# The second stage's weight jobs issued in the group that uses them, and another table of scores with O's second half transposed in the ninth step

## The reference

```
s = attention(xn)          # 32 heads of 16, q and k layer-normed, ALiBi slopes, causal, softmax, output projection
g = silu(ffn(xn))          # (silu(xn @ Wg) * (xn @ Wu)) @ Wd, inner size 1792
out = x + s * g            # Wg, Wu, Wd are integers 0..15: (w - zero) * scale per group of 128 rows
```

## Time and profile before

| | |
|---|---|
| three timed runs | 1124.39, 1126.78 (median), 1127.07 us |
| the profiled execution | 1119.51 us, of which the span 1117.7 us lies between its first and last instruction |
| PE, DVE, ACT, POOL busy over the span | 1039.0, 933.7, 722.6, 465.6 us |
| second stage, first to last exponentials | 193.0 to 705.3 us |
| mean granted clock of TensorE | 0.978 of 2.4 GHz |

### The profile page before, as it was taken

The page is one execution under the profiler, slowest core; times in us unless marked ns, Lnnn a source line. Parts: engine busy times, 40 slices in busy tenths (PEclk is TensorE's granted clock), DMA queues, the critical chain, the costliest instruction groups (busy, mean ns, idle before and its releaser), DMA issues. The chain is left out here.

```text
span 1117.7 us, 18980 instructions
## 1 busy us (share of the span) xinstructions
PE 1039.0 (93%) x6242; PEld 639.5 (57%) x6242; DVE 933.7 (84%) x2162; ACT 722.6 (65%) x1152; POOL 465.6 (42%) x554
## 2 busy tenths in 40 slices
PE   5999987998999999989999999899999999999995
PEld 4788764433344343433444333577778778777874
DVE  6778897887888787878889885579989998998896
ACT  3666655675767666666667668567747766774774
POOL 2566545221111111111121112039946864994686
PEclk9999999999999998999999999899999999999997
DMA  6254862543544544464454343100120011012001
GB/s 214 70 158 137 220 149 78 154 123 64 142 109 109 129 78 97 90 142 109 95 125 94 103 87 106 39 1 0 40 75 1 1 49 66 1 39 76 1 1 38
DMA packets 98584, 95.32 MB, mean 85 GB/s; under 512 B 28030, under 2 KB 80950, under 8 KB 98486
## 3 DMA queue, kind: packets, MB, share of 16 engines
q1 hardware_dynamic: 96854, 93.72, 32.7%
q10 hardware_dynamic: 1632, 0.39, 0.2%
HBM read 72.45 MB, written 21.23 MB: 84 GB/s over the span
## 5 line engine op out<-in xcount | busy, mean ns | idle before, releaser
L896 ACT ACTIVATE pr<-pair 128x1024 f32<-128x1024 f32 (+3 forms) x384 | 296.6, 813 | 168.1 <-PE pair L1017 90.7
L279 DVE CUSTOM_DVE_ANT_0 bank<-bank,sg 128x384 f32<-128x384 f32 (+3 forms) x488 | 231.4, 517 | 73.4 <-PE bank L289 72.1
L1538 PE MATMUL pair<-xc_lo,w_gu 128*128 128x512 f32 x448 | 182.6, 408 | 4.1 <-DVE xc_lo L1374 4.1
L1539 PE MATMUL pair<-xc_hi,w_gu 128*128 128x512 f32 x448 | 176.5, 394 | 0.0
L282 DVE TENSOR_REDUCE mx<-bank 128x1 f32<-128x512 f32 x240 | 150.5, 684 | 6.0 <-PE bank L289 3.7
L1386 DVE SCALAR_TENSOR_TENSOR gate<-pair,sgu,gate 128x512 f32<-128x512 f32 x168 | 124.5, 741 | 27.0 <-PE pair L1539 25.4
L1177 POOL TENSOR_TENSOR yt<-yt,tmp 128x512 f32<-128x512 f32 x96 | 124.2, 1314 | 0.0
L289 PE MATMUL bank<-ks,qs 108*128 108x512 bf16 (+3 forms) x384 | 116.2, 335 | 5.6 <-DMA ks<-in_krows 5.0
L1012 PE MATMUL pair<-s_sb,xin_c 111*128 111x512 bf16 (+3 forms) x384 | 97.8, 338 | 12.0 <-DMA s_sb<-dt 9.2
L289 PE MATMUL bank<-xin_c,s_sb 108*128 108x512 bf16 (+3 forms) x344 | 106.0, 341 | 3.1 <-DMA xin_c<-in_krows 3.0
L1012 PE MATMUL pair<-qs,ks 111*128 111x512 bf16 (+3 forms) x384 | 97.1, 337 | 12.7 <-DMA qs<-dt 11.0
(11 more groups left out here) (122 smaller groups left out, 2166.5 us busy)
## 6 DMA issues: line engine op xcount, KB each, us to landing
stk<-parts SPq DMA_DIRECT2D x16, 768.0 KB, 5.7
zst<-in_z_all SPq DMA_DIRECT2D x24, 448.0 KB, 4.0
sst<-in_w_all SPq DMA_DIRECT2D x24, 448.0 KB, 5.7
xin_c<-in_x SPq DMA_DIRECT2D x32, 256.0 KB, 3.3
s_sb<-stk SPq DMA_DIRECT2D x96, 64.0 KB
xin_c<-stk SPq DMA_DIRECT2D x96, 64.0 KB
qs<-stk SPq DMA_DIRECT2D x96, 64.0 KB
ks<-stk SPq DMA_DIRECT2D x96, 64.0 KB
```

The lines of the kernel that those rows point to most:

```text
L279: dve.tensor_tensor_reduce(out=src, in0=src, in1=tri[:, 512 - w:512], scale=1.0, scalar=-3.0e38, op0=ALU.add, op1=ALU.max, accum_out=dst). ...
L896: act.activation(pr[e % 3][:, 2 * p:2 * p + 2, 0:w], pair[p][:, :, 0:w], ACT.Exp, scale=SCALE)\
L1538: pe.matmul(GB[j % 4], w, xc_lo[:, k, :], start=True, stop=False)
L1539: pe.matmul(GB[j % 4], w, xc_hi[:, k, :], start=False, stop=True).then_inc(gu_done, 1)
```

## The change

Three things change, all in the second stage. The table `PLAN` is another one: the group's own pieces come first, D1 moves from the first place of the eleventh step to the last of the tenth, O0 from the fourth step to the last place of the ninth, O1 from the tenth step to the twelfth, and five small pieces stand in the group's very last place. The weight jobs move: each group `i > 0` issues the pair of job `3 ip + s` at its start on SP, and an odd group after it that of job `3 ip + 2`, in front of its loads; the conversions stand in front of the fourth step's exponentials, and in odd groups also in front of the ninth's; POOL's jobs follow. And since `ot` is now still waiting for its transposes when the upper half's output is finished, `copy_o` of the upper half waits for O0.

```diff
         PLAN = (
-            "4u 5u 3", "4u", "6u",
...
+            "2 2", "2", "4u",
...
+            "", "O1", "0 0 1 1 0",
...
-        JOB_AT, JOB1_AT = 6, 2
+        JOB_AT, JOB2_AT = 3, 8
...
                 def body(i, s, ip, last):
-                    if s == 1:
-                        half_job(ip, 2)
-                    if not last:
-                        half_job(*((ip, 1), (ip + 1, 0))[s])
-                    else:
+                    if i > 0:
+                        half_job(ip, s)
+                    if last:
...
+                    if s == 1:
+                        half_job(ip, 2)
                     if last is None:
...
                 def body(i, s, ip, last):
-                    if s == 1:
-                        job(ip, 1)
-
                     pool.wait_ge(m_free, number(i, of_kind["own"][-1]) + 1)
...
-                    job(ip, (0, 2)[s])
+                    job(ip, s)
...
+                    if s == 1:
+                        job(ip, 2)
...
                 def copy_o(i, k):
-
+                    if k == 0 and i > 0:
+
+                        act.wait_ge(m_full, number(i, "O0") + 1)
...
-                        if e == JOB1_AT and s == 1:
-                            convert(ip, 1)
                         if e == JOB_AT:
-                            convert(ip, (0, 2)[s])
+                            convert(ip, s)
+                        if e == JOB2_AT and s == 1:
+                            convert(ip, 2)
```

More of the change, by code:

```diff
@@ L217, in build @@
         PLAN = (
-            "4u 5u 3", "4u", "6u",
[L219 to L229, removed]
+            "2 2", "2", "4u",
+            "2 6u", "3 3", "5u 7u",
+            "3 7u", "6u", "5u 5u",
+            "4", "3 7 4", "6u 4u",
+            "4u", "4 4 6", "7",
+            "D0 6", "5 7u", "6u",
+            "5", "7u 7", "5 6",
+            "", "", "4u 7",
+            "5u 5", "6", "O0",
+            "", "", "D1",
+            "1", "", "0 1",
+            "", "O1", "0 0 1 1 0",
         )
```

## The result

| | before | after |
|---|---|---|
| timed runs, median | 1126.92 us (1124.39 to 1129.4) | 1169.56 us (1167.78 to 1172.15) |
| ratio, 95% interval | 1 | 1.038 (1.035 to 1.0411) |
| profiled execution | 1119.51 us | 1169.37 us |
| mean of groups 1 to 14 | 32.5 us | 36.1 us |

The changed kernel is 3.8% slower: 42.6 us by the medians, 49.9 us by the two profiled executions. Forecast were 1176 us and 49 us more.

The account below looks back on a forecast made before the run. PE was taken to set the pace inside a group before; after the change, a ring through SP sums to 35.0 us, 36.2 with the clock, 3.5 above 32.72: 49 us more over 14 periods, 1176 us, range 1130 to 1204.

Parts of the forecast that it names:

- The ring: Second stage, from group 1: group length is one round through SP, from first upper load to the next, 35.0 us.
- wait for the twelfth step's scores: On SP, lower loads wait for these scores after the upper loads: 0.6 us, about 1.2 in odd groups, average 0.9.
- pair, from v's issue until landed: The weight pair's issue behind v's load on SP and its landing: 6.4 us, with ends 4.8 and 8.2.
- fifth to eighth step, at full clock: These steps at PE's pace: 8.1 us, plus 0.3 for 640 more columns of pieces, 8.4 in sum.
- The pause of PE: PE stands still some 4 us once a group before the fifth step's scores, held by the fourth step's exponentials.
- rival 1: Pair lands in time, seam between groups goes: 30.2 us a group, 35 us less in all, 1092; chance 0.10.
- The clock: TensorE's clock falls with the pause: between 0 and 2.3 us, middle of 1.2 taken for every group.
- 14 periods: Second stage, first exponentials of group 0 to group 14's: 32.72 us each before, 3.5 more after, 49 in all.
- The gain from D1 and the later pieces lost in the ring: At the group's start, 0.8 to 2.1 us a group, lost because PE gets ahead and then waits longer.
- `copy_o`: ACT's wait for O0 while PE transposes: between 0 and 1.9 us, taken as 0.
- The second (1130): Stall half hidden: pair lands in 4.4 us, clock does not fall, 32.9 us a group, 3 us more; chance 0.10.
- The third (1208): Pauses add up: landing takes 7.8 us, clock low twice as long, 38.5 us a group, 81 more; chance 0.10.

Follow-up runs that it names:

- v apart: Changed kernel with v's load on a semaphore of its own, so the lower loads no longer count it: 1185.95 us, ratio 1.0582.
- the jobs alone: Changed kernel with the old table put back, so against the kernel before only the weight jobs moved: 1190.55 us, ratio 1.0579.
- the table alone: Kernel before with the new table and `copy_o`'s wait for O0, the weight jobs as they were: 1123.09 us, ratio 0.9974.
- the table and v apart: Kernel before with the new table, `copy_o`'s wait and v's load on its own semaphore, old weight jobs: 1106.36 us, ratio 0.9842.
- half the pair: Changed kernel loading only 448 of 896 columns of zeros and weights from the second job on: 1141.09 us, ratio 1.0174.

## Why the prediction was right, step by step

**The ring** was the right mechanism, shown from three sides: with the conversion later, with the pair earlier in SP's list and with half the bytes, the time falls to 1133, 1142 and 1141 us, each inside its range. The sum of 35.0 and 1.2 for the clock, 36.2, stands against 36.13 in the mean of groups 1 to 14. Its terms, in the turn from group 7's end into group 8 (rows of SP and ACT above), and in the mean of the 13 turns into groups 1 to 13 (the same rows of each turn):

| term | predicted | turn into group 8 | mean of 13 turns |
|---|---|---|---|
| issuing upper, lower, v | 15.4 | 16.1 (7.2 + 7.3 + 1.66) | 16.2 (7.8 + 7.6 + 0.8) |
| wait for the twelfth step's scores | 0.9; 1.2 odd | 1.25 (474.35 to 475.60) | 0.5 |
| pair, from v's issue until landed | 6.4 | 5.6 (484.54 to 490.10) | 5.8 |
| conversions | 1.7 | 1.7 | 1.7 |
| fourth step | 1.9 | 1.8 | 1.9 |
| fifth to eighth step, at full clock | 8.4 | 8.8 (of 10.4) | 8.8 (of 9.6) |
| until the next load | 0.3 | 0.2 | 0.2 |
| clock | 1.2 in every group | 1.6 | 0.8 |
| sum | 36.2 | 37.1 | 36.0 |

The 8.8 us of the fifth to eighth step are what the six of these groups take in which the fifth step has 3.3 us. In the mean the issuing and the fifth to eighth step are longer than predicted, by 0.8 and 0.4 us, and the pair's landing, the clock and the wait for the twelfth step shorter, by 0.6, 0.4 and 0.4. That these nearly cancel is luck; each of them is small beside the 3.5 us that were forecast. v's issue of 1.66 us, 1.1 more than in the earlier trace rows, belongs to this turn: most others have 0.55. The landing was taken from all 24 transfers of before. Those of them that went out behind v with nothing right behind them, one in each odd group from 1 to 13, landed in 4.4 to 5.7 us, 4.7 in the median, and those with the upper loads right behind them in 5.5 to 7.8: the pair of the changed kernel is of the first kind. Its median is 4.8 us and not 5.7, and with the lower loads behind it, in the kernel with the pair earlier, it is 5.9.

The forecast's own range does not follow from its two terms as it stands: 35.0 - 1.0 and 35.0 + 1.0 + 2.3 are 34.0 and 38.3 us, not 34.3 and 38.0, which makes 1145 to 1205 us instead of 1149 to 1201. The time measured lies inside either.

**The pause of PE** was put at 4 us in one piece with the wait on the exponentials at 3 to 5. It is 2.8 us at the most there, because the wait for v has taken 1.5 us a group before it; the two together are 3.6 us a group (46.9 in 13). That wait is the step missing in the prediction: rival 1 names the lower loads and v as late for the first lower piece, and I did not look up what the semaphore counts. In the changed kernel it costs nothing of its own, since it lies inside ACT's wait, and by splitting the pause it even saves: the groups are 1.2 us shorter than with v apart.

**The clock.** Taking the middle between 0 and 2.3 for every group was near in the sum and not in its kind: the clock is below 1.00 in ten of the groups 1 to 14, and the fifth step is longer for it in eight, by 1.6 us in seven and 0.9 in one; in groups 1 and 9 the low stretch ends before that step. The direction agrees with the Trainium skill (TensorE: Matmul & The Clock Gate, Why this matters for your kernels), which advises against idle gaps of PE between bursts of matmuls. The kernel before pays for a fallen clock too, in six of its groups 1 to 14, and from 224 to 690 us its mean is 0.97 like that of the changed kernel. So the clock's share belongs into the length of the ring, as the sum has it, but the changed kernel does not run at a lower mean clock than the one before.

**14 periods** was the right number, of other groups than those that the 32.72 was read from. Groups 1 to 14 stall, and group 14 too has the pair in front of it: 37.18 us against 29.67. In these 14 groups the mean rises from 32.53 to 36.13 us, 3.60 a group where 3.5 were forecast, 50.4 us in all; everything else is 0.5 us faster, which gives the 49.9 of the profiled executions. Between the starts of groups 0 and 14 alone it is 42.9 us (500.9 less 458.05).

**The gain from D1 and the later pieces lost in the ring** was right: with the old jobs and v apart the table is worth 1.6% (0.9842), 18 us or 1.0 us a group, of which 11 us are D1's; with v counted as before it is worth nothing that can be told (0.9974), where the prediction's estimate of 0.8 to 2.1 us a group did not see the wait for v; in the changed kernel it shows only as the 2% against the jobs alone, beside the smaller and split pause and the shorter way from the eighth step to the twelfth. **`copy_o`** at nothing: it stands in the kernel with the table alone too, whose time shows no loss; by itself it was not tried.

**The rivals.** The first (1092) fell with the pair's place, but the kernel with the table and v apart comes to 31.5 us a group, 1.0 of the 2.5 us that the rival assumed, with the jobs where they were. The second (1130) needed a clock that does not fall; half the pair is near that case, with 33.7 us a group and a clock of 0.99, where the rival had 32.9. The third (1208) is what the jobs alone come closest to, with 37.4 us a group.

## What to carry to other kernels

In an in-order DMA queue a transfer's place in the list is its start time. Before moving a use, add up the issues that stand ahead of the load, and see how early the use asks for it; here it cost 46 us that a weight pair stood behind a group's loads and was asked for in front of the fourth step. Asking three steps later, or issuing it ahead of the lower loads, takes most of that away (ratios 1.0076 and 1.0146 instead of 1.038). Look up everything that a semaphore counts, since a reader of one transfer waits for all that share it; giving v its own was worth 16.7 us where that wait was on the path. And price a pause of TensorE with what follows it: the matmuls behind it may run at the lower clock, so removing a wait that only splits a pause can lose time.

## What the runs showed that was not expected

- Removing a wait of 1.5 us a group made the kernel slower, from a ratio of 1.038 to 1.0582 (mean clock from 224 to 690 us 0.97 and 0.91), and adding 280 needless matmuls to that made it faster (1.0337, clock 1.00).
- The issue of v's load on SP took 1.66 us in the turn shown and 1.74 and 1.88 in two others, 0.55 in the rest. Other single issues are long too, as that of `sst` in the earlier trace rows (1.53). Why was not tried.
- Why the clock falls in some groups of the changed kernel and not in others, at pauses of like length, stays open.
